# The scalar engine, not the sync engine, issues the two copies of the rotary queries inside SBUF

## The reference, cut to what matters

```
c_q, c_kv = x @ Wq_down, x @ Wkv_down                       # latent 64
q_c = (c_q @ Wq_up)   -> 128 heads x 4                      # "content" query
q_r = (x @ Wq_rope)   -> 128 heads x 64                     # "rotary" query
k_c, v_c = (c_kv @ Wk_up), (c_kv @ Wv_up) -> 128 heads x 4
k_r = x @ Wk_rope                                           # 64, one for all heads
scores = (q_c . k_c + q_r . k_r) / sqrt(4 + 64)
out = softmax(scores) @ v_c ;  x = x + gate * (out @ Wo)
```

## Time and profile before

| | |
|---|---|
| median of 3 runs | 2240.83 us (2239.58 to 2241.4) |
| the profiled execution's own time | 2241.55 us |
| its span, first to last instruction | 2239.7 us |
| busy: PE, DVE, ACT, POOL | 2144.8, 1650.2, 1431.8, 1461.2 us |
| second attention's first exponential | at 815.6 us |
| first exponential of unit 96 | at 1806.7 us |

### The profile page before, as it was taken

One profiled execution on the slowest core, in us unless ns is written; L12 is line 12 of the kernel. 1 busy time (PEld: TensorE's weight loads), 2 busy tenths in 40 slices (PEclk: granted clock), 3 DMA queues, 4 the chain that ended last, 5 costly groups with the idle time before them and its releaser, 6 DMA issues.

```text
span 2239.7 us, 42472 instructions
## 1 busy us (share of the span) xinstructions
PE 2144.8 (96%) x11276; PEld 1644.0 (73%) x11276; DVE 1650.2 (74%) x2903; ACT 1431.8 (64%) x2901; POOL 1461.2 (65%) x1621
## 2 busy tenths in 40 slices
PE   7999999999999999999999999999999999999978
PEld 4788888888886657777777777777777776666656
DVE  6787787787876667777777777777777777787764
ACT  3433443443434678888888888888888865555532
POOL 4666666766762468888888888887888821354334
PEclk9999999999999999999999999999999999999998
DMA  7100100100031352222222222222222223344341
GB/s 242 47 21 29 47 19 28 47 19 28 19 93 44 102 174 74 72 66 72 75 62 71 76 66 71 72 74 62 71 76 71 66 73 98 109 125 124 109 131 38
DMA packets 138989, 165.80 MB, mean 74 GB/s; under 512 B 30261, under 2 KB 72917, under 8 KB 138916
## 3 DMA queue, kind: packets, MB, share of 16 engines
q1 hardware_dynamic: 135076, 152.31, 23.8%
q0 software_dynamic: 3840, 12.59, 2.0%
HBM read 101.52 MB, written 29.10 MB: 58 GB/s over the span
## 4 chain that ended last, share of the span: by engine, by line
PE 58%; DVE 9%; SPq 9%; issue 8%; POOL 7%; DMA 5%; ACT 3%; POOLq 0%; ACTq 0%; DVEq 0%
PE bank L2128 6%; PE bank L2130 6%; PE bank L2129 6%; PE bank L2551 6%; PE bank L2564 5%; PE bank L2571 5%; DMA q<-qc_d 3%; PE bank L2483 3%; PE bank L2481 3%; PE bank L2482 3%; POOL pH L912 2%; SPq L569 2%; POOL pH_late L912 2%; PE bank L2603 2%; PE bank L2593 2%
## 5 line engine op out<-in xcount | busy, mean ns | idle before, releaser
L1909 DVE TENSOR_REDUCE mcol<-bank 128x1 fp32r<-128x512 f32 x1024 | 693.2, 688 | 335.4 <-PE bank L2551 327.9
L2551 PE MATMUL bank<-km,q 128*128 128x512 f32 x1024 | 417.5, 409 | 30.5 <-DMA q<-qc_d 22.5
L2564 PE MATMUL bank<-q,k 128*128 128x512 f32 x1024 | 418.2, 408 | 7.6 <-DMA k<-kc_d 7.6
L2571 PE MATMUL bank<-q,k 128*128 128x512 f32 x1024 | 404.4, 395 | 0.0
L2551 PEld LDWEIGHTS bank<-km,q 128*128 128x128 f32 x1024 | 317.6, 310 | 99.2 <-issue 48.7
L1398 ACT ACTIVATE pT<-bank 128x512 f32<-128x512 f32 x512 | 296.5, 600 | 143.9 <-PE bank L2571 134.0
L1398 ACT ACTIVATE x<-bank 128x512 f32<-128x512 f32 x512 | 295.7, 599 | 56.3 <-PE bank L2571 54.1
L912 POOL TENSOR_TENSOR pH<-x,pH 128x512 f16<-128x512 f32 x192 | 228.9, 1212 | 128.2 <-ACT x L1398 128.2
L2564 PEld LDWEIGHTS bank<-q,k 128*128 128x128 f32 x1024 | 192.3, 188 | 94.1 <-issue 44.0
L912 POOL TENSOR_TENSOR pH<-pT,pH 128x512 f16<-128x512 f32 x192 | 220.1, 1167 | 10.8 <-ACT pT L1398 10.7
L2571 PEld LDWEIGHTS bank<-q,k 128*128 128x128 f32 x1024 | 193.9, 189 | 32.4
(11 more groups left out here) (369 smaller groups left out, 4808.6 us busy)
## 6 DMA issues: line engine op xcount, KB each, us to landing
q<-q SPq DMA_DIRECT2D x256, 128.0 KB, 2.3
wst<-in_L_attn_Wq_rope SPq DMA_DIRECT2D x64, 256.0 KB, 3.3
o_d<-ost SPq DMA_DIRECT2D x63, 256.0 KB, 3.3
st_q<-in_L_attn_wq SPq DMA_DIRECT2D x8, 1024.0 KB, 7.6
st_wo<-in_L_attn_wo SPq DMA_DIRECT2D x8, 1024.0 KB, 5.2
km<-kc_d SPq DMA_DIRECT2D x256, 32.0 KB
q<-qc_d SPq DMA_DIRECT2D x256, 32.0 KB
k<-kc_d SPq DMA_DIRECT2D x256, 32.0 KB
```

The source lines that it names most:

```text
L1909: dve.tensor_reduce(mcol[:, k % 2, i % 4, i // 4:i // 4 + 1], bank[4 + i % 2][:], AX.X, ALU.max, negate=True)\
L2551: pe.matmul(bank[4 + i % 2][:], q2[:, k % 4, h, i % 4:S:4], km[:, b, h], start=True, stop=True).then_inc(max_mm, 1)
L2564: pe.matmul(bank[s % 4][:], k1[:, k % 2, t], q1[:, k % 4, h], start=True, stop=False)
L2571: pe.matmul(bank[s % 4][:], k2[:, k % 2, h, t], q2[:, k % 4, h], start=False, stop=True).then_inc(scores1, 1)
```

## The change

The wait for `q2_hi` and the two copies leave SP's period. ACT's period gets them, behind the exponential of slot 0: it waits until its own queries' high part is written, then issues the two transfers, then goes on with the exponential of slot 1. The `sem_inc` on a spare semaphore is what carries the wait, as in `hold`. Sizes, source, destination and the semaphores raised are the same, and so is the number of transfers (256).

```
@@ SP, period(u, k), v = u + 2
                         sp.dma_start(q2[r:r + 1, (k + 2) % 4, h]..., mrow[h:P:32, k % 2]).then_inc(m_loaded[k % 2], 16)
-                    hold(q2_hi, v + 1)
-                    for h in range(2):
-                        r = slice(ROPE * h, ROPE * h + ROPE)
-                        sp.dma_start(q1[r, (k + 2) % 4, h].bitcast(F32), q2[r, (k + 2) % 4, h].bitcast(F32)).then_inc(q1_hi[k % 2], 16)
@@ ACT, period(u, k, pair), for s in range(8)
                         act.activation(PT[k % 2][:, s], bank[s % 4][:], ACT.Exp, scale=...).then_inc(exp1, 1)
+                    if s == 0 and exists(u + 2, UNITS):
+                        act.wait_ge(q2_hi, u + 3)
+                        act.sem_inc(spare, 1)
+                        for h in range(2):
+                            r = slice(ROPE * h, ROPE * h + ROPE)
+                            act.dma_start(q1[r, (k + 2) % 4, h].bitcast(F32), q2[r, (k + 2) % 4, h].bitcast(F32)).then_inc(q1_hi[k % 2], 16)
                     if s in CAST_BEHIND and exists(u, HALVED):
```

## The result

The changed kernel takes 2264.8 us (median of 4 runs, 2263.38 to 2267.25) beside 2241.11 for the kernel before (4 runs, 2239.58 to 2242.85): ratio 1.0107, 95% interval 1.0089 to 1.0124, or 23.7 us slower. The forecast was 2276, 35.5 us slower, with a range of 2238 to 2318. Its profiled execution took 2263.56 us, with a span of 2261.5.

A forecast was written before the change was run, and what follows sets the result against it. Two nearly equal loops, through POOL (20.53 us per pair) and SP (20.72), were taken to bound units 0 to 95. 2241.55 + 39.5 (recovered 5.8 included) - 4 = 2277.05, or 2276.3 on the median's footing; range 2238 to 2318.

The forecast's parts named there:

- The POOL loop: Units 0 to 95: even unit's exponentials, POOL's subtractions, PE's sum; 20.53 us per pair of units, rising to 21.47.
- The delay d: ACT, exponential 1 starts 0.94 us late behind the two issues; in even units of the stage with casts it counts fully.
- SP's relief: SP loses 1.29 us of issuing per period: worth 5.8 us in units 0 to 95, 4 us in the last units.
- No price of d without casts: Units from 96 on: ACT idles 1.16 us after exponentials 0 to 3, so 0.94 costs nothing; otherwise 30 us.
- One issue at a time: Rival: ACT's issues queue with SP's L609, giving 2303.7 or 2333.5 us; chance 0.27, including an issue dearer on ACT.
- Hidden issue: Rival: ACT's sequencer issues while exponential 0 runs, d is 0 and only gains remain, 2231.1 us; chance 0.13.

The follow-up runs named there:

- odd-only: ACT issues the copies in odd periods only, SP in even ones as in the kernel before: 2229.76 us, 0.9946 of the kernel before.
- even-only: ACT issues the copies in even periods only, SP in odd ones as in the kernel before: 2272.73 us, 1.0139 of the kernel before.
- the version with exponential 6: The changed kernel with ACT's wait and two copies behind exponential 6 in place of exponential 0: 2225.34 us, 0.9933 of the kernel before.
- the moved split: POOL's split of the rope weights moved from behind the second subtraction to behind the sixth: changed kernel 2202.88 us, kernel before 2231.68 us (0.9950).
- the bare wait: Kernel before, SP keeping both copies; ACT gets only the wait and spare increment behind exponential 0, no transfer: 2243.02 us, ratio 1.0009.
- SP's other order: Kernel before with both copies still on SP, but ahead of its wait for DVE's transpose: 2224.87 us, ratio 0.9919.

## Why the prediction was right, and where its sizes were off

**The POOL loop as the place of the loss** held. The odd-only and even-only versions, the version with exponential 6 and the moved split each change the lateness or the length of this loop, and the length of a pair follows. ACT's load, traffic and the bare wait were the other accounts; each has an experiment against it.

**The delay d** was given as 0.94 and is 0.87. The two issues took 1.12 us on ACT against 1.17 on SP, and exponential 1 came 0.17 us behind them, not 0.20. Over 48 pairs the difference is 3.4 us. The two issues were to take 0.53 to 0.60 us each; they take 0.47 and 0.62.

**The loop took only 0.76 of it.** The pair went from 20.53 to 21.29. POOL's first subtraction moved by 3.13 - 2.27 = 0.86, but from there to PE's sum it is 9.6 us in place of 9.72. The prediction said that nothing else in the loop becomes shorter. In the kernel before, DVE's cast of the rope weights took 0.80 us, all of it beside POOL's first two subtractions, and these took 2.48 us; in the changed kernel POOL starts only 0.2 us before the cast ends. The cast takes 0.43 and the two subtractions 2.35. First the kernel before, then the changed one, DVE's timeline and POOL's:

```profile
1252.62 0.80 DVE L1788 CAST wr_hi<-wst 128x512 fp32r<-128x512 f32 x1
```

```profile
1251.97 2.48 POOL L912 TENSOR_TENSOR pH<-x,pH 128x512 f16<-128x512 f32 x2 [2.59 <-ACT x L1398]
```

```profile
1266.16 0.43 DVE L1790 CAST wr_hi<-wst 128x512 fp32r<-128x512 f32 x1
```

```profile
1266.38 2.35 POOL L908 TENSOR_TENSOR pH<-x,pH 128x512 f16<-128x512 f32 x2 [3.27 <-ACT x L1394]
```

Over 48 pairs this is some 6 us (9.72 less 9.60). With d it explains the stage: +30.5 where +39.5 was forecast. The medians over the even units are the same as in these rows; they are 2.48 wherever exponential 1 isn't late (odd only, wait alone, exponential 6, SP's other order) and 2.36 in the even-only version. That the cast and the subtraction slow each other is read from this and was not tried by itself. The pair came to 21.3 us where 21.5 was forecast, and POOL's idle time before an even unit to 3.2 us (152.7 in 47) where 3.6 was. Two sums of the prediction are off by 0.1 us (48 x 20.53 less 991.05 is -5.6, and 48 x 0.2 is 9.6), which changes nothing.

**SP's relief** in the stage with casts was right: PE's 22.5 us of waits for the query load are gone. It is worth less than the 5.8 us reckoned: the three versions that relieve SP and leave the POOL loop alone (odd only, exponential 6, SP's other order) take 987.1, 987.6 and 986.4 us for the stage, 3.5 to 4.7 less than before. In the last units the relief was mis-sized: 4 us with a bound of 5.0, measured 10.9. The bound came from one kind of wait in one window. The kernel before has one unit there of 15.26 us among its neighbours' 10.45 (exponential 0 at 1900.11 and 1915.38), with PE held ahead of a maximum for 3.04 us of "issue" time, that is for nothing that the profile shows:

```profile
1900.71 3.04 issue
1903.75 0.78 PE bank L2551
```

In the three versions where SP still issues both odd copies behind the maxima (even only, wait only, POOL's split alone) this unit is long too, but 11.5 to 11.7 us; in the changed kernel and the one with the copies behind exponential 6 it is 10.45. How much of the 4.8 us belongs to SP and how much to that one execution stays open. The unit also lies in the window of the earlier trace rows that was to keep its 129.6 us: units 96 to 107 take 124.7 in the changed kernel.

**No price of d without casts** fits: a unit that nothing disturbs takes 10.45 us in both kernels, exponential 1 being late in one (units 102 to 104, for instance). The last units as a whole are 319.7 us, and 316.6 in the version with exponential 6; that is about as far apart as two executions of one version, so a price of up to 3 us isn't excluded, where 30 was the rival.

**One issue at a time** is out. SP's two issues at 1263.49 lie right across ACT's, and take what they took alone:

```profile
1263.49 1.19 SPq L609 DMA_DIRECT2D q<-mrow  x2
```

The Trainium skill's rule of a shared generator that one sequencer locks ("Perfetto Trace Analysis", section "DMA Instruction — HWDGE (DVE, Sync)") shows no price in these rows: 0.47 and 0.62 us on ACT, 1.19 for two on SP, at the same moment. It is so in 118 such meetings of the changed kernel. Where SP issues nothing beside them, ACT's first issue takes the same 0.47 (six places there) and its second the same 0.62 (79 places behind exponential 6). Some price may show elsewhere: behind exponential 6 ACT's second issue takes 0.77 us in the 22 places where it meets two of SP's other transfers.

**Hidden issue** was wrong for this place and right as a mechanism. Behind exponential 0 the wait ends only with L1356, the sequencer's lead is gone, and exponential 0 covers 0.49 us of what follows. Behind exponential 3 the wait has long been met, the sequencer is some 1.1 us ahead, and 1.1 us of issues cost nothing. A wait long met isn't enough by itself: behind exponential 6 the lead is only 0.05 to 0.15 us, and with POOL's split in its old place exponential 7 comes 0.15 us late, where nothing waits for it. The prediction's argument against the rival, the late wait and the order, names the condition that failed behind exponential 0.

## What to carry to other kernels

In this kernel a transfer's issue on a computing engine cost what the engine's own sequencer had no lead for. So put it a few instructions after the data it needs are ready, where the profile shows the sequencer ahead, and away from the load that something waits for. Before moving work off a queue, try another order in that queue; by itself that gave as much here as a second queue (0.9919 beside 0.9933), and with POOL's split moved all but 5 us of it. When two loops are within 1% of each other, find both and change both: the moved copies alone lost 1.1%, the moved split alone won 0.5%, the two with the copies at a better place won 2.9%.

## What the runs showed of the hardware

- ACT's issue of a 128 KB copy inside SBUF takes 0.47 us for the first and 0.62 for the second of a pair; SP's takes 0.53 and 0.59.
- ACT's sequencer starts an issue about 1 us ahead of the instruction in front of it in the program (1231.75 against 1232.78), where no wait holds it; behind exponential 6 it is 0.05 to 0.15 us.
- Issues on SP and ACT at the same moment each take what they take alone (1.19 us for two, 0.47 and 0.62).
- With two copies of 128 KB issued at the same time, a 32 KB load that PE waits for lands in 3.87 to 5.42 us in place of 2.66 to 3.44.
- PE, which shows 19.91 us busy for a pair of units in the kernel before, does the same matmuls in 19.54 in the fastest version.
- DVE's cast of a 128x512 tile takes 0.80 us where it runs wholly beside POOL's subtractions and 0.43 where it meets them for 0.2 us.
